# Chunked linear-attention recurrence on one core: sorted gram rows for the selector matmuls, and another placing of leaf and GpSimd work within a chunk

## The reference, cut to what matters

```python
def step(S, t):
    q_t, k_t, v_t, a_t, b_t = t
    y = jnp.einsum('bhvk,bhk->bhv', S, k_t)
    err = y - v_t
    S = a_t[..., None] * S - (b_t[..., None] * err)[..., None] * k_t[:, :, None, :]
    o = jnp.einsum('bhvk,bhk->bhv', S, q_t)
    return (S, o)
...
o = _delta_scan(q, k, v, a, beta)
mu = jnp.mean(o, axis=-1, keepdims=True)
var = jnp.mean(jnp.square(o - mu), axis=-1, keepdims=True)
o = (o - mu) * jax.lax.rsqrt(var + LN_EPS) * ln_g + ln_b
g = jax.nn.sigmoid(x @ Wg).reshape(b, t, H, D)
o = (o * g).reshape(b, t, H * D)
return o @ Wo
```

## Time and profile before

| | us |
|---|---|
| three runs | 3706.5 median (3702.6 to 3709.7) |
| the profiled execution | 3708.6, its span 3706.9 |
| TensorE busy | 3351.2 (90%) |
| VectorE busy | 2638.9 (71%) |
| ScalarE busy | 1461.7 (39%) |
| GpSimd busy | 1213.1 (33%) |
| selector matmuls, line 1302 | 523.0 busy, 2176 records |

### The profile page before, as it was taken

How to read it: one execution, slowest core, us unless ns; L and a number is a source line. 1 busy time by engine, 2 the same in 40 slices (tenths; PEclk the granted TensorE clock), 3 DMA queues, 4 the chain that set the end, 5 groups by cost and what they waited for, 6 DMA issues and landing times. The chain is left out here.

```text
span 3706.9 us, 50282 instructions
## 1 busy us (share of the span) xinstructions
PE 3351.2 (90%) x15480; PEld 2358.2 (64%) x15480; DVE 2638.9 (71%) x5876; ACT 1461.7 (39%) x3126; POOL 1213.1 (33%) x1388
## 2 busy tenths in 40 slices
PE   5999996699999999999999999999999999978888
PEld 3555553577767777777776767777777777634444
DVE  5777775688787787877878787888888778522222
ACT  3666664244333343434344333344433334311110
POOL 1666665233333232333333333333333333300000
PEclk9999998798989998989999989999999999979999
DMA  2655656322211121211122211122211121020000
GB/s 74 247 226 205 258 206 239 73 52 41 42 35 36 37 57 36 46 36 35 36 53 41 44 38 36 35 53 42 45 37 35 36 45 26 13 83 17 17 17 17
DMA packets 431900, 255.18 MB, mean 69 GB/s; under 512 B 400080, under 2 KB 414128, under 8 KB 416944
## 3 DMA queue, kind: packets, MB, share of 16 engines
q1 hardware_dynamic: 431680, 252.42, 24.5%
HBM read 147.40 MB, written 104.99 MB: 68 GB/s over the span
## 5 line engine op out<-in xcount | busy, mean ns | idle before, releaser
L744 POOL TENSOR_TENSOR B_WT<-B_WT,B_G 128x128 f32<-128x128 f32 (+2 forms) x224 | 145.1, 648 | 1316.1 <-issue 1316.1
L245 DVE SCALAR_TENSOR_TENSOR A_acc<-A_psY,A_w,A_acc 128x410 f32<-128x410 f32 (+1 forms) x720 | 419.3, 637 | 156.0 <-ACT A_acc L285 156.0
L1031 ACT ACTIVATE B_WL<-B_psT 128x128 f32<-128x128 f32 (+2 forms) x480 | 150.3, 313 | 950.7 <-PE B_psT L1405 950.6
L1302 PE MATMUL B_ring<-B_OWN,B_source 128*128 128x64 f32 (+2 forms) x2176 | 523.0, 405 | 0.8 <-DVE B_OWN L868 0.8
L1302 PEld LDWEIGHTS B_ring<-B_OWN,B_source 128*128 128x128 f32 x2176 | 376.3, 217 | 84.5 <-issue 53.0
L949 DVE TENSOR_TENSOR B_NC<-B_NC,B_psM 128x256 f32<-128x256 f32 x480 | 200.5, 418 | 255.5 <-PE B_psM L1426 200.0
L345 PE MATMUL A_psY<-A_xT,A_w 128*128 128x413 f32 (+1 forms) x960 | 347.2, 510 | 9.1 <-PE A_psAG L351 7.7
L202 POOL TENSOR_TENSOR A_outs<-A_outs,A_acc 128x410 f32<-128x410 f32 (+1 forms) x240 | 229.3, 987 | 254.6 <-ACT A_outs L293 254.6
L345 PEld LDWEIGHTS A_psY<-A_xT,A_w 128*128 128x128 f32 x960 | 180.2, 189 | 165.5 <-issue 164.2
L1426 PE MATMUL B_psM<-B_BD,B_WL 128*128 128x128 f32 x1536 | 257.7, 312 | 12.5
L1426 PEld LDWEIGHTS B_psM<-B_BD,B_WL 128*128 128x128 f32 x1536 | 211.1, 210 | 86.2 <-ACT B_WL L1031 85.6
(11 more groups left out here) (196 smaller groups left out, 6550.4 us busy)
## 6 DMA issues: line engine op xcount, KB each, us to landing
scr<-A_outs SPq DMA_DIRECT2D x48, 1024.0 KB, 5.5
B_KQ<-scr SPq DMA_DIRECT2D x96, 512.0 KB, 6.5
scr<-A_outag SPq DMA_DIRECT2D x32, 1024.0 KB, 8.1
A_xc<-nbeta SPq DMA_DIRECT2D x18, 1024.0 KB, 8.6
scr<-A_x SPq DMA_DIRECT2D x16, 1024.0 KB, 7.6
B_A<-scr SPq DMA_DIRECT2D x32, 512.0 KB, 4.5
B_C<-scr SPq DMA_DIRECT2D x32, 512.0 KB, 4.5
B_G<-scr SPq DMA_DIRECT2D x32, 512.0 KB, 4.5
```

What stands on the lines that cost most here:

```text
L245: nc.vector.scalar_tensor_tensor(a, y, w[:, s, col:col + 1], a, ALU.mult, ALU.add)\
L1302: last = mm(dst[:, :, :, leaf::2], source[:, R * leaf + r:R * leaf + r + 1].to_broadcast([128, 128]), grams_own[:, R * leaf + t0:R * leaf ...
```

## The change

**Sorted rows.** `OWN` has one buffer in place of two. ScalarE copies its key grams to `KS` and its query grams to `QS` (a new function `sort_own`, twice a chunk, two copies of 512 elements), with a row `t` of a leaf pair contiguous. The selector matmuls read these and write contiguous columns, since the rows in `X`, `WX` and `FQ` are now ordered by leaf parity, head, leaf pair. `kk` groups its runs: in place of ten matmuls a half, six. The order of elements changes with it in `row_pairs` (three multiplies in place of two), `leaf_solution`, `decayed_w`, `decayed_q` and `centered_copy`.

**Other slots.** The table `leaf_jobs` and the branches of the other engines are written anew. TensorE, jobs after the merge of a leaf: `own` of the second half from 1 to 0, `qk` from 0, 0, 1, 2, 4 to 1, 1, 3, 3, 4, `kk` from 3 to 2 and from 12 to 11, `own` of the next chunk from 10 to 9, the first `update` from 13 to 12, second `wo` half from 11 to 13. VectorE: the next chunk's `decays` from leaf 13 to 9, its `mask_own` from 11 to 10, `row_pairs` from 13 to 12, its three `leaf_solution` parts from behind leaf 15 to leaves 13, 14 and 15. ScalarE: `leaf_diagonals` of the next chunk from 14 to 11, `ktok` copies from 12 to 11. GpSimd: the gate in four parts and the decayed queries in two, each set between the scalings.

The diff, cut to its core:

```diff
-    out = {0: [("qk", 0), ("qk", 1)], 1: [("qk", 2)], 2: [("qk", 3)], 4: [("qk", 4)], 5: [("oc", 0)], 6: [("oc", 1)],
...
+    jobs = {0: [("own", 1, 0), ("own", 1, 1)],
+            1: out and [("qk", 0), ("qk", 1)],
...
-        OWN = sb("OWN", [128, 2, J // 2, 2, H, 2 * R])
+        OWN = sb("OWN", [128, J // 2, 2, H, 2 * R])
+        KS, QS = sb("KS", [128, 2 * R, H * J // 4]), sb("QS", [128, 2, 2 * R, H, J // 2])
...
         def by_row(ap):
-            return ap.rearrange("p h (j r) -> p r h j", r=R)
+            return ap.rearrange("p h (n l r) -> p r l h n", l=2, r=R)
...
-            def decayed_q(o):
+            def decayed_q(o, n):
...
-                tt(FQ.rearrange("p (r h j) -> p h j r", r=R, h=H), leaves(Q[:, o % 2]), leaves(F[:, o % 2]), ALU.mult)\
-                    .then_inc(fq.sem, 1)
+                tt(FQ.rearrange("p (r l h n) -> p r l h n", r=R, l=2, h=H)[:, r], by_row(Q[:, o % 2])[:, r],
+                   by_row(F[:, o % 2])[:, r], ALU.mult).then_inc(fq.sem, 1)
...
+                gates = lambda *parts: [gate(g - 2, n) for n in parts if g >= 2]
                 scale_right(g, 1)
+                gates(0)
                 scale_left(g, 1)
-                if g >= 2:
-                    gate(g - 2)
+                gates(1)
...
                 for j in (5, 7, 9, 11, 13):
+                    if g and j < 9:
+                        decayed_q(g - 1, (j - 5) // 2)
...
+                wait(dve, nlc, i, 1)
+                ps = rows(take_bank(dve, g if h else g - 1, "kk", h, 0))
+                tt(xr[:, 3], ps[:, 1], ar[:, 1], ALU.mult).then_inc(nl.sem, 1)
+                tt(xr[:, 4], ps[:, 2], rr, ALU.mult).then_inc(nl.sem, 1)
+                wait(dve, nlc, i, 2)
+                ps = rows(take_bank(dve, g if h else g - 1, "kk", h, 1))
+                tt(xr[:, 5], ps[:, 1], ar[:, 2], ALU.mult).then_inc(nl.sem, 1)
...
+            def sort_own(i):
+
+                h, g = i % 2, i // 2
+                pairs = OWN[:, 4 * h:4 * h + 4]
+                wait(act, ow, g, 2 * h + 2)
+                wait(act, nl, i - 1, 3)
+                wait(act, nlc, i - 1, 2)
+                copy(KS[:].rearrange("p t (h n) -> p t h n", h=H), pairs[:, :, 0].rearrange("p n h t -> p t h n")).then_inc(ks.sem, 1)
+                wait(act, yv, g - 2, 5)
+                copy(QS[:, g % 2, :, :, 4 * h:4 * h + 4], pairs[:, :, 1].rearrange("p n h t -> p t h n")).then_inc(qs.sem, 1)
...
                         for leaf in range(2):
-                            last = mm(dst[:, :, :, leaf::2], source[:, R * leaf + r:R * leaf + r + 1].to_broadcast([128, 128]),
-                                      grams_own[:, R * leaf + t0:R * leaf + t0 + m], start=True, stop=True)
+                            last = mm(dst[:, :, leaf], source[:, R * leaf + r:R * leaf + r + 1].to_broadcast([128, 128]),
+                                      rows[:, R * leaf + t0:R * leaf + t0 + m], start=True, stop=True)
```

243 lines of the change are left out of this document (127 added, 116 removed).

## The result

The changed kernel takes 4016.24 us (median; 4014.94 to 4022.41) against 3708.11 (3702.64 to 3715.09) on the same chip: **1.0833 times the time before, 95% interval 1.0811 to 1.0855**. The profiled execution has a span of 4012.9 us for 3706.9, at a granted clock of 0.898 for 0.925. The forecast was 3863 us with a range of 3655 to 3960: the direction was right, the loss twice as large as reckoned, and outside the range.

A forecast was written before the change was run, and what follows sets the result against it. TensorE looked like the bound, but each leaf step was set by TensorE, VectorE or loop latency. Step terms summed to +5.05 us a chunk, over 31 turns +157 on the 3706.5 us median: 3863 us, range 3655 to 3960.

The forecast's parts named there:

- step 2: Leaf step 2 of a chunk: one 512-wide VectorE operation fewer and no gate, near 3.4 us for 5.1, -1.7.
- step 5: Leaf step 5: half the query product and two scalings fall on part 2 of the leaf solution, +2.1 us.
- step 6: Leaf step 6: one y operation more on an engine that is full, +0.6 us.
- step 10: Leaf step 10: two masks come in and the deviation waits behind ScalarE's sort copies, 6.0 us for 3.4, +2.6.
- step 11: Leaf step 11: falls to the latency of a four-leaf merge, 3.4 us for 3.9 (odd chunks 5.6), -1.35 on average.
- Step 12: Leaf step 12: ScalarE's rest copy ends 2.2 us in, 5.8 us for 3.1 (odd chunks 6.55), +1.0 on average.
- step 14: Leaf step 14: part 2 of the leaf solution comes in on VectorE, 4.4 us for 3.1, +1.3.
- The turnover: Step 15, taken with step 0: two VectorE parts leave, TensorE's 11.88 us stays, -0.3 us together.
- step 3: Leaf step 3: row pairs wait for ScalarE's pair copies, then three multiplies and a mask, 5.0 us for 4.5, +0.5.
- Step 7: Leaf step 7: TensorE starts ahead, -0.5 us.
- The rival of the clock: Rival, chance 0.09: after longer waits in steps 10 and 12, a quarter of turnover's TensorE work at 1.2 GHz, 3956 us.
- Steps 1 and 9: Step 1: GpSimd pieces fall on the decays, 6.2 us for 5.4, +0.8. Step 9: next chunk's decays, 4.0 for 3.1, +0.9.

The follow-up runs named there:

- warm_fit: Changed kernel plus idle-time matmuls that nobody waits for, 6 calls behind slot 1 and 8 behind slot 5: 3888.79 us, 1.0492 of the kernel before.
- mask_first: Changed kernel with VectorE's mask_gram(g, 1) ahead of row_pairs in slot 3: 4001.91 us, 1.0783 of the kernel before.
- the three edits: Changed kernel with mask ahead of row_pairs, deviation ahead of the sort, and decayed_q in two stride-free pieces behind block_decays: 3821.49 us, 1.0303 of the kernel before.
- all edits: Changed kernel with mask first, deviation first, decayed_q in two stride-free pieces, 6 and 3 idle-time calls behind slots 1 and 5, 48-column variance matmuls: 3742.13 us, 1.0073.
- var_wide: Kernel before with the eight variance matmuls of slot 9 taking 48 equal columns in place of one: 3683.75 us, 0.9938.
- dq_early: Kernel before with sorted q rows, 48-column variance matmuls, and GpSimd's decayed_q ahead of scale_left(g, 3), behind WT of leaf 3: 3651.89 us, 0.9831.

## Why the prediction was right in direction and short by half

**Prices that held.** The sort copies took 1168 and 1151 ns (forecast 1050; the earlier trace rows was the right neighbour); the strided query product 2397 ns a half (forecast 2100); a gate quarter 780 (600). The 256-wide selectors fell from 0.50 us a record to 0.24 (eight records in 1.89 us). All selectors together lost 5.3 us a chunk (546.3 to 377.5 us in the groups by shape) and not 8; among others the kk ones of step 3 now run at the lower clock (3.25 us for twelve records, 1.75 in warm_fit). That this relief would not show in the time was right, and so was the reading that VectorE's new work and holds decide several steps: 2, 5, 6, 10, 11, 12 and 14 came within 0.5 us of their terms. (Step 12's own sum gives 2.1 us and not 2.2 for the rest copy, which changes nothing.)

**The turnover** with step 0 was better than forecast by 1.8 us. I let TensorE's 11.88 us stay, and it fell to 8.59 in chunk 14. I had overlooked two moves in the new table: the block `gram` 3 went from the chunk's start to slot 4 (four records of 256 columns fewer, 1.6 us), and the second `update` from slot 14 to 13 (2.1 us). I had put the gain at 1.4 us at most, which TensorE's old load would have allowed.

**The step that failed most** is step 3, "three multiplies to 3.9 and a 0.68 mask before the next leaf: 5.0", +0.5 where +4.24 was measured. It has two errors. I priced kk and the gram at full clock, 2.5 us, and they took 5.3 (the earlier trace rows had already shown step 5 of the kernel before at 0.64). And I put the mask in front of the *next* leaf, while the merge of leaf 3 itself reads what the mask writes: the wait is inside the step, and TensorE is on both sides of it. mask_first alone takes 2.6 us off step 3, the idle-time calls alone 2.4, and both together, with decayed_q out of the way, 4.25: step 3 is then what it was before the change, 4.30 us.

**Step 7** was to lose 0.5 "since TensorE starts ahead" and gained 1.5. All of it is clock: 4.57 us with the calls, and 5.01 with the three edits, which shorten step 5 and so TensorE's standstill in it.

**The rival of the clock** named the right mechanism in the wrong place, and its chance of 0.09 was far too low. I looked for its price in the turnover, which holds the most TensorE time; there the clock stayed at 1.00 in chunk 14. What ran slow in the changed kernel came behind standstills, and those of steps 1 and 5 I had myself worked out: 3.3 us of TensorE work in a step of 6.2, and at most the 4.98 us of the earlier trace rows in a step of 8. Between the first and the last row sum the lower clock was granted for 416 us before, 682 after, and 299 in warm_fit. A standstill is not the only thing that a fall can follow: in step 4 of the kernel before, TensorE is busy for 6.36 of 6.83 us and the clock is at 0.81.

**Steps 1 and 9** were each 1 us short. I had priced VectorE's six decays of step 9 as in step 1 of before, 1.9 us in all (0.39 us each, overlapping a little). The timeline of step 9 after the change, GpSimd and VectorE:

```profile
1975.48 0.80 POOL L743 TENSOR_TENSOR B_P<-B_P,B_G 128x256 f32<-128x256 f32 x1
1976.24 0.79 POOL L743 TENSOR_TENSOR B_Q<-B_Q,B_G 128x256 f32<-128x256 f32 x1
```

```profile
1975.11 0.66 DVE L811 TENSOR_TENSOR B_B<-B_A 128x128 f32<-128x128 f32 x1
1975.69 0.83 DVE L813 TENSOR_TENSOR B_B<-B_RR,B_A 128x128 f32<-128x128 f32 x1
1976.44 0.84 DVE L815 TENSOR_TENSOR B_F<-B_F,B_A 128x128 f32<-128x128 f32 x1
1977.31 0.40 DVE L817 TENSOR_TENSOR B_F<-B_F,B_A 128x128 f32<-128x128 f32 x1
```

Beside GpSimd's two scalings the decays take 0.83 and 0.84 us, behind them 0.40. For step 9 I had left this hold out, although shows it. For step 1 I had counted all four GpSimd pieces, but at 2.6 us together; they took 3.2 in chunk 14, and the step 6.73 us for the 6.2 forecast. The rest of the 1 us is the clock again. In 18 of 28 chunks step 1 is 6.73 us; in the other 10 it is 7.9 in the mean, and there the `own` grams, which the change moved in front of leaf 1's transposes, run at the lower clock. Chunk 14, then chunk 16:

```profile
1926.17 1.99 PE L1323 MATMUL B_ring<-B_KQ,B_KL 128*128 128x256 f32 x8
```

```profile
2108.32 3.51 PE L1323 MATMUL B_ring<-B_KQ,B_KL 128*128 128x256 f32 x8
```

**What is left.** With all edits the changed kernel stands 1.35% above var_wide (1.0073 against 0.9938). Between these two a chunk differs by +1.66 us in step 1, -2.18 in step 2, -0.58, +0.73 and -0.35 in steps 4, 6 and 7, +1.77, +0.80 and +0.84 in steps 9, 10 and 12, +1.12 in step 14 and -2.03 in the turnover, 1.7 us in all with the steps left out here (79.32 and 80.99). This is what none of the edits removed. Of the forecast's terms, those of steps 2, 3, 4, 6, 7, 12 and 14 fit it within 0.5 us; steps 1 and 9 are twice theirs, step 10 is far below its own since the deviation no longer waits, and the turnover is 1.7 us better. Whether another order of the new slots would mend the rest was not tried.

## What to carry to other kernels

When work is taken from the busiest engine of a loop with a latency chain, or moved about on it, look for where it will now stand still, and price whatever it does right behind each standstill at the lower clock: here filling two standstills gave 3.4% of the time, more than any other single edit. Compare the two job tables entry by entry: two moves that I overlooked stand beside a turnover that beat its term by 1.8 us. Before a step is moved, follow every consumer of what its engine makes behind it, also within the same step, and ask which of them sits on the chain. And test a reordering together with its companions: mask_first alone gained 0.5%, because the time it freed was taken at once by a GpSimd instruction that held VectorE.

## What the runs showed of the hardware

- The clock that TensorE is granted can be bought with matmuls whose results nobody reads: 14 calls a chunk, 6.6 us of TensorE time in its standstills, gave back 4 us a chunk.
- Eight matmuls of one column cost as much as eight of 48 columns (16 records in 1.84 and 1.88 us), and step 11 behind them fell from 4.64 to 3.92 us in the mean: in the kernel before the lower clock is granted in 12 of 28 of these steps (1.4 us in the mean of all), in var_wide in none.
- GpSimd's product of two operands read one element at a time costs 4.7 ns an element (2397 ns for 512), in runs of four 2.5 (1280 ns), although the writes of the second were the scattered ones. A VectorE product of 64 elements beside the first took 2.18 us for 0.21. The Trainium skill (GPSIMD Engine Reference, Performance pitfalls for Q7 kernels) puts such reads at about half more per element; measured was 1.9 times.
- The hold is not always one instruction for one: beside GpSimd scalings of 0.8 us several VectorE products in a row took 0.83 to 0.92 us in place of 0.39, and the whole gate held a single one for all of its length (2.52 us beside 2.37). VectorE's products with one operand in PSUM were not held: in dq_early one of 512 elements took its usual 0.68 us within GpSimd's 2.37.
